# A two-layer tanh recurrence on one core: layer 0's third state tile multiplied in three bf16 parts, its rests moved to VectorE, and the order of a slot changed

## The reference

```python
def layer(x, h0, Wx, Wh, b):
    xW = einsum('ntd,dh->nth', x, Wx) + b
    h_t = tanh(h_{t-1} @ Wh + xW_t)        # 1024 steps, one after another
x = x + layer(x, cond_1024, L0_cond_Wx, L0_cond_Wh, L0_cond_b)
x = x + layer(x, cond_1024, L1_cond_Wx, L1_cond_Wh, L1_cond_b)
```

## Time and profile before

| | |
|---|---|
| median of three runs | 2058.94 us |
| the profiled execution | 2059.2 us |
| its span, from first to last instruction | 2057.4 us |
| PE busy | 2046.2 us (99%) |
| DVE busy | 1837.9 us (89%) |
| ACT busy | 1539.9 us (75%) |
| POOL busy | 444.0 us (22%) |

### The profile page before, as it was taken

One profiled execution on the slowest core, in us unless ns is written; L12 is line 12 of the kernel. 1 busy time (PEld: TensorE's weight loads), 2 busy tenths in 40 slices (PEclk: granted clock), 3 DMA queues, 4 the chain that ended last, 5 costly groups with the idle time before them and its releaser, 6 DMA issues.

```text
span 2057.4 us, 224159 instructions
## 1 busy us (share of the span) xinstructions
PE 2046.2 (99%) x98384; PEld 1952.7 (95%) x98384; DVE 1837.9 (89%) x12254; ACT 1539.9 (75%) x7426; POOL 444.0 (22%) x2054
## 2 busy tenths in 40 slices
PE   8999999999999999999999999999999999999999
PEld 7999999999999999999999999999999999999998
DVE  5999999999999999999999999999999999999997
ACT  5777777777777777777777777777777777777776
POOL 3222222222222222222222222222222222222221
PEclk9999999999999999999999999999999999999999
DMA  3000000000000000000000000000000000000000
GB/s 106 28 24 28 24 27 25 26 25 26 26 25 26 25 27 24 28 24 28 24 28 24 28 24 28 24 28 24 28 24 28 24 28 24 28 24 27 25 26 18
DMA packets 111995, 56.59 MB, mean 28 GB/s; under 512 B 12432, under 2 KB 111008, under 8 KB 111520
## 3 DMA queue, kind: packets, MB, share of 16 engines
q1 hardware_dynamic: 111168, 53.53, 9.0%
q10 hardware_dynamic: 576, 1.18, 0.2%
q0 software_dynamic: 32, 0.02, 0.0%
HBM read 37.90 MB, written 16.78 MB: 27 GB/s over the span
## 4 chain that ended last, share of the span: by engine, by line
PE 99%; DMA 1%; issue 0%; DVE 0%; ACT 0%; ACTq 0%; SPq 0%
PE ps_rec L303 44%; PE ps_rec L324 33%; PE ps_xw L279 22%; DMA wx<-wx_in 0%; DMA wh<-wh_in 0%; PE ps_rec L376 0%; DVE zt L541 0%; ACT h L445 0%; SPq L255 0%; ACTq L498 0%; ACTq L497 0%; DVE x_out L581 0%; DVE z L550 0%; SPq L254 0%
## 5 line engine op out<-in xcount | busy, mean ns | idle before, releaser
L303 PE MATMUL ps_rec<-wh,h 128*32 128x128 f32 x33024 | 1271.8, 273 | 4.1 <-ACT h L445 2.7
L445 ACT ACTIVATE h<-z 128x16 f32<-128x16 f32 x4066 | 709.2, 217 | 481.7 <-DVE z L550 475.4
L324 PE MATMUL ps_rec<-wh_part,h 128*32 128x128 bf16 x48792 | 1047.4, 219 | 1.5 <-issue 1.5
L303 PEld LDWEIGHTS ps_rec<-wh,h 128*32 128x32 f32 x33024 | 832.5, 109 | 79.6 <-ACT h L445 9.2
L324 PEld LDWEIGHTS ps_rec<-wh_part,h 128*32 128x32 bf16 x48792 | 890.1, 97 | 15.4 <-issue 1.9
L541 DVE STREAM_TRANSPOSE zt<-ps_rec 128x64 f32<-128x64 f32 x4096 | 778.8, 228 | 94.0 <-PE ps_rec L303 14.2
L214 POOL TENSOR_TENSOR h<-h 128x16 f32<-128x16 f32 x2032 | 430.1, 212 | 1589.4 <-DVE h L214 1589.4
L434 ACT ACTIVATE ps_rec<-xw,mask 128x128 f32<-128x128 f32 x2040 | 731.9, 359 | 9.5 <-issue 1.0
L550 DVE TENSOR_REDUCE z<-zt 128x16 f32<-128x48 f32 x4066 | 650.6, 199 | 0.9
L214 DVE TENSOR_TENSOR h<-h 128x16 f32<-128x16 f32 x2034 | 357.3, 176 | 110.7 <-ACT h L445 2.8
L279 PE MATMUL ps_xw<-wx,x_pe 128*32 128x128 f32 x8248 | 409.9, 273 | 0.5 <-issue 0.5
(11 more groups left out here) (23 smaller groups left out, 22.3 us busy)
## 6 DMA issues: line engine op xcount, KB each, us to landing
x_pe<-x_t SPq DMA_DIRECT2D x256, 64.0 KB, 1.9
x_dve<-x_t SPq DMA_DIRECT2D x256, 64.0 KB, 2.0
out_t<-x_out SPq DMA_DIRECT2D x256, 64.0 KB, 1.7
wh<-wh_in SPq DMA_DIRECT2D x1, 1024.0 KB, 5.2
wx<-wx_in SPq DMA_DIRECT2D x1, 1024.0 KB, 8.2
wx<-wx_in ACTq DMA_DIRECT2D x1, 512.0 KB, 5.0
wx<-wx_in SPq DMA_DIRECT2D x1, 512.0 KB, 4.8
wh<-wh_in SPq DMA_DIRECT2D x1, 512.0 KB, 7.9
```

The costliest lines, as they stand in the source:

```text
L303: mm = pe.matmul(rows(ps_rec[l][n % 2], g), h_step(l, n - 1)[:, k, :], wh[l][:, k, g * P:(g + 1) * P], start=False, stop=k == KC - 1 and n ...
L324: mm = pe.matmul(ps_rec[l][n % 2][32 * g:32 * g + 32, cols], h_bits(l, n - 1)[:, k, :], wh_part[l][:, i, to + cols.start:to + cols.stop], ...
L445: act.activation(h_of(l, n)[:, tiles, :], src[:, tiles, :], ACT.Tanh).then_inc(h_count(l, n)[0], 1)
```

## The change

- `KB = (3, 2)`: layer 0's tile 2 is in parts as well, all of its 128 columns (`PART_COLS`). POOL makes a fifth tile of `wh_part`, last. PE waits for it once, after `head(7)` and ahead of the loop.
- Layer 0's rests: DVE takes the first rest of tiles 0, 1, then the first rest of tile 2 (behind the second tanh), then the second rest of tiles 0, 1. POOL takes the second rest of tile 2. PE waits for the two separately (`split_done` has one more pair of semaphores for layer 0).
- Layer 1's rests: both on POOL; DVE has none of them.
- PE's slot becomes `head` (layer 0's parts, both projected tiles of the slot, layer 1's whole tile 2) and `tail` (layer 1's whole tile 3, its parts, layer 0's whole tile for the next step). The loop runs from `tail(7)` to `head(8)` and so on. `PROJECT` gives each slot two tiles of one layer.
- The blocks of the state and the lowest block summed change for the third of four steps (`BLOCKS`, `LOWEST`). In one step of four the second half of layer 0's sum takes four blocks instead of three.
- `rec_done` is counted once a step, not once a half. ACT's `pass_xm`, `copy` and `seed` for the projections move to places between layer 0's tanh and layer 1's.

```diff
-KB = (2, 2)
+KB = (3, 2)
+PART_COLS = ((P, P, P, 0), (P, P, 0, 0))
...
-PROJECT = (((0, 3), (1, 0)), ((1, 1), (1, 2)), ((1, 3), (0, 0)), ((0, 1), (0, 2)))
-BLOCKS = ((0, 1, 2), (1, 0, 2), (2, 1, 3), (3, 1, 2))
-LOWEST = (0, 0, 1, 1)
+PROJECT = ((0, (2, 3)), (1, (0, 1)), (1, (2, 3)), (0, (0, 1)))
+BLOCKS = ((0, 1, 2), (1, 0, 2), (2, 0, 1), (3, 1, 2))
+LOWEST = (0, 0, 0, 1)
...
             def recur_parts(l, n):
...
+                for k in range(KB[l]):
+                    cols = slice(0, PART_COLS[l][k])
+                    if k % 2 == 0:
+                        pe.wait_ge(*split_count(l, n - 1, k // 2))
...
-            def slot(s):
+            def head(s):
                 if s < T:
                     recur_parts(0, s)
...
-                projection(s, 0)
+                projection(s)
                 if (n := number(1, s)) is not None:
...
-                    recur_whole(1, n)
+                    recur_whole(1, n, range(KC - 1))
+
+            def tail(s):
+
+                if (n := number(1, s)) is not None:
+                    recur_whole(1, n, range(KC - 1, KC))
                     recur_parts(1, n)
...
-                projection(s, 1)
-                if s < T:
+                if s + 1 < T:
                     recur_whole(0, s + 1)
...
-            for s in range(PARTED):
-                slot(s)
+            for s in range(PARTED - 1):
+                head(s)
+                tail(s)
+            head(PARTED - 1)
             pe.wait_ge(s_wpart[0], PARTS * KB[0])
             with pe.Fori(0, (T - PARTED) // RING, 1):
-                for s in range(PARTED, PARTED + RING):
-                    slot(s)
+                for s in range(PARTED - 1, PARTED - 1 + RING):
+                    tail(s)
+                    head(s + 1)
+            tail(T - 1)
             for s in range(T, T + LAG):
-                slot(s)
+                head(s)
+                tail(s)
...
         # scalar: slot(s)
                 if s < T:
                     tanh(0, s)
+                if t == 0 and 0 <= r - 1 < NG:
+                    pass_xm(r - 1)
                 if t == 1 and 3 <= r + 1 < NG + 1:
                     act.sem_inc(seed0_done, -1)
+                if t == 1 and 2 <= r + 1 < NG:
+                    copy(0, r + 1)
                 if t == 2 and 0 <= r - 1 < NG:
                     act.sem_inc(xm_done, -1)
                     copy(1, r - 1)
+                if t == 2 and 2 <= (c := r + 2) < NG + 2:
+                    ...
+                        seed(0, c).then_inc(seed0_done, 1)
...
         # gpsimd
-            for l, k in POOL_MAKES:
+            for l, k in ((0, 0), (0, 1), (1, 0), (1, 1), (0, 2)):
...
             for l, n in ORDER:
                 if is_split(l, n):
...
+                    mine, done = (rest_done[1], n + 1) if l else (late_done, n + 2 - PARTED)
+                    tiles = HALVES[0] if l else slice(2, 3)
+                    if l:
+                        pool.wait_ge(*h_count(l, n, 0))
+                        rest(pool, l, n, 1, tiles).then_inc(mine, 1)
+                    pool.wait_ge(mine, done)
+                    rest(pool, l, n, 2, tiles).then_inc(split_count(l, n, 1 - l)[0], PAIR if (l, n) == (0, PARTED - 1) else 1)
...
         # vector
-            def rest_first(l, n):
-                if is_split(l, n):
-                    dve.wait_ge(*h_count(l, n, 0))
-                    rest(dve, l, n, 1, HALVES[0]).then_inc(rest_done[l], 1)
+            def rests(n):
+                if is_split(0, n):
+                    dve.wait_ge(*h_count(0, n, 0))
+                    rest(dve, 0, n, 1).then_inc(rest_done[0], 1)
+                    dve.wait_ge(*h_count(0, n, 1))
+                    rest(dve, 0, n, 1, slice(2, 3)).then_inc(late_done, 1)
+                    dve.wait_ge(rest_done[0], n + 2 - PARTED)
+                    rest(dve, 0, n, 2).then_inc(split_count(0, n, 0)[0], PAIR if n == PARTED - 1 else 1)
...
                 if n0 is not None:
-                    rest_first(0, n0)
+                    rests(n0)
...
-                if n1 is not None:
-                    rest_first(1, n1)
```

More of the change, by code:

```diff
@@ L209, in x_of, with rest @@
             return xs[n // S4 % 2][:, :].rearrange("p (k s b) -> p s k b", s=S4, b=B)[:, n % S4]
-        def rest(eng, l, n, part, tiles):
+        def rest(eng, l, n, part, tiles=HALVES[0]):
             step, to, of = h_step(l, n), h_cols(n, part), h_cols(n, part - 1)
             return eng.tensor_tensor(step[:, tiles, to], step[:, tiles, of], h_bits(l, n)[:, tiles, of], ALU.subtract)
[L216 to L234, removed]
         @block.sync
@@ L294, in recur_whole @@
                     pe.wait_ge(begun[0], 1)
-                tiles = range(in_parts(l, n), KC)
-                for k in tiles:
+                tiles = [k for k in range(KC) if in_parts(l, n, k) < P]
+                for k in only:
+                    if k not in tiles:
+                        continue
+                    cols = slice(in_parts(l, n, k), P)
                     if (l, n) == (0, 0):
@@ L302, in recur_whole @@
                     for g in range(QG):
-                        mm = pe.matmul(rows(ps_rec[l][n % 2], g), h_step(l, n - 1)[:, k, :],
-                                       wh[l][:, k, g * P:(g + 1) * P], start=False,
-                                       stop=k == KC - 1 and not in_parts(l, n), skip_group_check=True,
+                        out, state = rows(ps_rec[l][n % 2], g)[:, cols], h_step(l, n - 1)[:, k, :]
+                        if cols.start:
+                            out, state = out[0:B, :], h_of(l, n - 1)[:, k, :]
@@ L306, in recur_whole @@
+                        mm = pe.matmul(out, state, wh[l][:, k, g * P:(g + 1) * P][:, cols], start=False,
+                                       stop=k == KC - 1 and is_whole(l, n), skip_group_check=True,
                                        tile_position=(0, 32 * g))
-                if not in_parts(l, n):
-                    mm.then_inc(rec_done[l], 2)
+                if is_whole(l, n) and only[-1] == KC - 1:
+                    mm.then_inc(rec_done[l], 1)
             def recur_parts(l, n):
-                if not in_parts(l, n):
+                if is_whole(l, n):
@@ L321, in recur_parts @@
                     for i in range(PARTS):
                         for g in range(QG):
[L323 to L326, removed]
+                            at = k * D + g * P
@@ L327, in recur_parts @@
+                            mm = pe.matmul(rows(ps_rec[l][n % 2], g)[:, cols], h_bits(l, n - 1)[:, k, :],
+                                           wh_part[l][:, i, at:at + P][:, cols], start=False,
+                                           stop=k == KB[l] - 1 and i == PARTS - 1, skip_group_check=True,
                                            tile_position=(0, 32 * g))
[L328 to L334, removed]
+                mm.then_inc(rec_done[l], 1)
@@ L335, in projection @@
+            def projection(s):
+                l, tiles = PROJECT[s % S4]
                 c = (s - S4) // S4 if l else (s + 6) // S4
                 if 0 <= c < NG or l == 0 and s < T:
-                    if k == 0 and l == 0:
+                    if tiles[0] == 0 and l == 0:
                         if c == 2:
@@ L471, in slot @@
                     tanh(1, n)
-                if t == S4 - 1 and r < NG:
-                    pass_xm(r)
                 if s % PAIR == 0 and s:
```

109 lines of the change are left out of this document (42 added, 67 removed).

## The result

| | before | after |
|---|---|---|
| median, us | 2058.9 | 2079.2 (2077.26 to 2079.69, four runs) |
| ratio, 95% interval | | 1.0098 (1.008 to 1.0115) |
| span of the profiled run | 2057.4 | 2077.9 |
| PE / DVE / ACT / POOL busy | 2046.2 / 1837.9 / 1539.9 / 444.0 | 2063.6 / 1897.6 / 1526.2 / 659.2 |

The kernel became slower by 1.0%; 1.2% faster was forecast. The time lies outside the range of 2008 to 2062. The granted clock is full in both. Of the experiments' executions, one of e2 (2566.9) and one of e9 (2276.0) ran at a lower granted clock (0.75 and 0.85); they are left out of the ratios and move the medians given by less than 0.1.

The account below looks back on a forecast made before the run. PE bounded the kernel before; after the change the latency loops would. Loops 1.952 plus 6 ns gave 1.958 a slot against 1.983, -25.4 us over 1016 slots; with +1.2 at the start, 2059.2 became 2035.0, range 2008 to 2062.

Parts of the forecast that it names:

- PE's prices of a tile: PE time per tile: 0.218 us for a whole or projected tile, 0.168 for one in parts.
- The three loops: Latency loops through layer 0's parts, layer 1's whole tiles and layer 1's parts: 1.952, 1.949 and 1.948 a slot.
- rival C: POOL's wait on itself makes layer 1's parts slower; at x = 0.15, 2.02 a slot and 2101 us; chance 0.14.
- x: POOL's wait on itself between layer 1's two rests: taken as 0.08, bounded by 0.03 and 0.21.
- Tile 2's rest: Layer 0's first rest of tile 2 on DVE, ahead of the second rest; may push it by 0 to 0.02.
- PE's own work: PE's matmuls per slot: one whole tile becomes one in parts, 1.930, 0.050 less; 51 us if PE stays the bound.
- four-block sum: DVE's reduce in one step of four: 16 elements more, under 0.02, on the second tanh.
- late instructions: Rare late instructions: 3 ns a slot remain and some become uncovered; 3 to 8 ns, 6 taken.
- The start: POOL's fifth tile of parts is ready at 25.17 instead of 22.07; P0(8) ends at 26.5, against 25.33: +1.2 us.
- The gap behind the loop's entry: PE's fetch gap after entering the loop may stay or fall partly into the wait: 0 to -1.1, 0 taken.
- The port: DVE sums and POOL rests share one SBUF read port; spoke against the change, no time of its own beyond C's.
- D: Rival: late things add up (four-block reduce, tile 2's rest, uncovered fetches): 1.97 to 1.985 a slot, 2047 to 2062; chance 0.14.

Follow-up runs that it names:

- e2: Changed kernel with the loop's edge one tile earlier, between projected tiles and layer 1's whole tiles, two weight waits carried into the loop's body: 2060.6 us.
- e9: e2 with the two waits for layer 1's weights moved ahead of the loop, four-block sum kept: 2054.3 us (0.9982).
- e11: e10 with layer 0's second rest of tiles 0, 1 on POOL instead of DVE: 2118.0 us.
- e12: e10 with one projected tile left out of each loop slot, incomplete projection, only to time the loops: 2037.0 us.
- e10: e9 with three blocks instead of four in the second half of layer 0's sum every fourth step: 2042.0 us (0.9919).
- e4: Kernel before with only the loop's edge moved between layer 1's two whole tiles, order of work unchanged: 2093.1 us (1.0166).
- e1: Changed kernel with the loop's edge ahead of layer 0's parts, as before the change: 2079.3 us.
- e7: e1 with three blocks instead of four in layer 0's sum every fourth step: 2063.7 us.
- e6: Changed kernel, edge unchanged, with three blocks instead of four in layer 0's sum every fourth step: 2077.9 us.
- e3: Changed kernel with eight slots in a round of the loop instead of four, 127 branches instead of 254: 2067.6 us.
- e8: Kernel before with only the change's four-block sum in every fourth step of layer 0: 2065.8 us (1.0036).
- e5: e2 with three blocks instead of four in layer 0's sum every fourth step: 2059.5 us.

## Why the prediction was wrong

**What held.** PE's prices of a tile: layer 0's three tiles in parts take 1000.86 - 1000.36 = 0.50, and the two projected tiles 1001.30 - 1000.86 = 0.44, as forecast. The three loops: forecast 1.952, 1.949 and 1.948, measured 1.954 to 1.956 in the plain slots of the changed kernel. The links priced from far rows came out close: POOL's wait on itself is 0.078 to 0.079 in all 987 cases of the stretch from 60 to 2036 (0.08 taken, 0.03 to 0.21 bounded), so rival C's condition, x over 0.11, isn't met. Tile 2's rest does not push the second rest: the three take 0.39 where the dependent pair took 0.38. e11 and e12 test the loops from both sides. With both causes of the long slot taken out, e10 takes 2042.0, within the range and 7.0 above the forecast.

**The step that failed** is one sentence under PE's own work: that splitting layer 1's whole tiles across the loop's edge changes no order inside the loop. The order is the same, but a branch stands at the edge, and I costed it at nothing without naming what covers it. In the kernel before, the trace's list shows a branch of the same 0.21 with the next load 0.26 behind it as well. There two whole tiles, 0.44, were queued ahead of it, the load behind it came 0.44 after the held one, and its slot took the same 1.980 as the others: the delay fell into time for which PE had work. The change moved the edge to a place where PE's queue has just been held by the tanh, with one tile of 0.22 behind the hold: load held, +0.12 the branch, +0.26 the next load, 0.38 in all against 0.22 to 0.25 of work. e4 shows it alone (34.4 us in the kernel before), e9 against the changed kernel shows it undone (24.9 us less, the four-block sum still in), e1 and e7 show that the cover is what counts and not the old place: e7, with the edge in the old place and three blocks, is still 21.7 us above e10.

**A second term was mis-sized.** I priced the four-block sum at under 0.02, 16 elements by proportion. It takes 0.053 more (0.263 against 0.21). With the branch in the same slot it hid (e6: 1.3 us); with the branch covered it costs 12.3 (e10 against e9).

**A third, small.** For late instructions I took 6 ns a slot; the other three slots exceed their median by 12 on average (means 1.972, 1.961 and 1.968). The lists of waits of both kernels have such single stalls in like number (DVE's x_mid on ACT: 1.8 us in 8 times in either), so I read them as old ones that nothing covers any more; that is argued, not shown. e12, with more idle time on PE, gives 5 us of it back. What makes single instructions late was not tried.

**The sum again.** The plain slots' mean is 1.967, the fourth's 2.105, together 2.001 against the forecast 1.958: +0.043 x 1016 = +44 us, and 2035.0 + 44 = 2079. Branch and sum in one slot, 0.150 / 4 = 0.037, are the most of it: e10 without them is 37.2 us faster. Of these, taking out the branch's stall alone gives 24.9 (e9), the sum alone 1.3 (e6).

**The start.** P0(8)'s transpose came 0.96 later than before (26.52 against 25.56), with +1.2 forecast. PE waited for POOL's last part until 25.00, as said:

```profile
25.00 0.43 PE L279 MATMUL ps_rec<-wh,h 128*32 128x128 f32 x8 [1.68 <-POOL wh_part L505]
...
28.61 0.30 PE L279 MATMUL ps_rec<-wh,h 128*32 128x128 f32 x2 [1.26 <-issue]
```

The gap behind the loop's entry, which the prediction put down to missing instructions, stayed and grew (1.26 against 0.88; the trace says only that PE waited for nothing that it shows), and step 20 is 2.05 late instead of 0.96. I had taken 0 to -1.1 for it.

**The port.** The x_out sum did not stretch (182 ns on average, before 181; one of 987 took 214), and in the median it starts 0.127 after the reduce's start, as before, although POOL's second rest of layer 1 runs over its start. The 0.99 of the earlier trace rows beside the making of parts has no match in the steady slots, so no price of the rule that I weighed there could be seen here.

**Rivals and chances.** Slower had 0.14, all of it on POOL's own wait, and that mechanism was not the one. D had named the four-block reduce and uncovered stalls, but at 1.985 a slot at most, where the mean is 2.001. The branch was no rival at all: the diff showed it, in the one part of the change that I had not costed. Its cost in the old place was in the trace of before to be read, in PE's queue, where the first load of L324 after the edge came some 0.05 later than its like without costing anything. The Trainium skill has a rule nearby (Runtime: NRT & Kernel Launch, section "Instruction fetch mechanics"): a taken branch whose target is outside the loaded window makes the engine wait for a fetch. By e3, where the distance to the next load stays 0.26 with twice the body, what was paid here is not a cost that grows with the body, and no round of e3 shows such a fetch at the edge.

## What to carry to other kernels

A loop's edge is an instruction: find the branch in the engine's queue and add up the work that is queued between the last thing that held the queue and the branch. If that is less than the branch and its refill (0.38 from the hold to the next load here), the edge costs up to the difference every round (here 0.10 to 0.15 of 0.16); put it behind the longest stretch of work that waits for nothing. And when a change brings a kernel down to its latency loops, expect that delays which had been hidden are paid in full, as the four-block sum's 0.053 was in e9 (0.028 before, in e8): price those at their whole length.

## What the runs showed of the hardware

- A loop's branch on PE takes 0.207 to 0.208 us in nearly every round of every run. Where no semaphore holds it longer, the next weight load of the program starts 0.262 to 0.264 after the branch's start, with a body of 800 or of 1600 matmuls and loads (the kernel after, e3).
- POOL starts 0.078 after the semaphore that it waits for, whoever raised it (DVE, ACT or POOL itself); PE's load 0.05, DVE 0.03. Two POOL subtractions of which the second's wait is met already overlap by 0.04 (e11: 0.37 for two, of 0.21 and 0.20).
- DVE's reduce of 128x64 to 128x16 (four blocks) takes 0.263, that of 128x48 in the same place 0.21.
- In e2 and e5, a load that waits for more semaphores than one has a wait instruction of 0.051 ahead of it, and started 0.06 later than with one.
